# Attention: the swap of q's halves is begun before the store of the output three units old

## The chip, the cores and the metric

The kernel runs on one core of one Trainium2 chip. The metric is the device time of a whole execution in microseconds. Three runs of the kernel before took 2433.12, 2435.80 and 2437.37 us, so its median is 2435.8 us.

## The reference, cut to what matters

The input is x of shape 8 x 512 x 512. A layer norm goes ahead of each of two layers, and both are added to their input. The first is an attention with 16 heads of 128 columns, the second a feed-forward layer that works on the 128 best rows of every 1024. The change touches only the attention, of which these lines matter:

```python
q = _rope((x @ Wq).reshape(b, n, H, HD)); k = _rope((x @ Wk).reshape(b, n, H, HD))
v = (x @ Wv).reshape(b, n, H, HD)
# _rope, with t1, t2 = t[..., :half], t[..., half:]
return jnp.concatenate([t1 * cos - t2 * sin, t1 * sin + t2 * cos], axis=-1)
o = o_cmp * g_cmp[..., None] + o_slc * g_slc[..., None] + o_swa * g_swa[..., None]
return o.reshape(b, n, H * HD) @ Wo
```

In these inputs all 8 key blocks of a row are chosen, so the chosen attention is the causal one.

## The kernel before, in words

The work is cut into 128 units. A unit is one head of one batch: its 512 rows lie along the free axis and the 128 columns of the head on the partitions. `unit(p, k, j)` numbers them: pair p of heads (8 of them), 4 groups k, 4 units j in each.

A unit passes through a pipeline of three bodies on each engine; every engine has its program written out in this order.

- TensorE (`body`, L618): projects q and k of unit u (L600, 12 matmuls of 512 columns each), then computes the scores of unit u-1 (L643), turns the probabilities of unit u-2 (L657), projects v (L613) and multiplies the probabilities of u-2 with v into bank 6 (L678).
- ScalarE (`body`, L754): `output_out(u)` copies that product, which is unit u-3's output by the time it does so, from bank 6 into `o_sb` (L737). `evacuate(u, 0)` copies q from its bank into `s_full[0]` (L706); later `evacuate(u, 1)` does the same with k. Between these it mixes the probabilities (L743) and takes v (L751). After them come the exponentials, and two roundings into `qk_hi` (L713).
- SyncE (`body`, L492) issues the transfers. `swap(u, 0)` (L466) waits until q is in `s_full[0]` (L468) and writes its lower half of 64 partitions to the upper half of `s_swap[0]` (L469) and the upper to the lower (L470). `swap(u, 1)` does so for k. `store` (L472) waits for `output_out` (L479) and writes `o_sb` to `o_scratch` in DRAM (L480). Loads of weights, of v's weights and of gates go in at a few units in each pair of heads.
- GpSimd (`body`, L565): `turn(u, 0)` waits for q's swap and makes the rotation: times cosine (L555), swapped times sine (L556), sum (L559). `turn(u, 1)` does it for k. Then `low` (L563) makes the two low parts, q's first. These `qk_lo` and `qk_hi` are what the scores read one unit later.
- VectorE reads the scores, masks them, mixes the probabilities (L847, L863) and makes low parts.

One buffer is shared: `o_sb = s_swap[1]` (L401). The output is copied into the same tile that k's swap fills afterwards. So SyncE waits, between the store and k's swap, until the store has landed (`out_slot_free`, L505). Also, `evacuate(u, 0)` on ScalarE waits until GpSimd has made q's low part of unit u-1 (`lo_done[0]`, L705), since both use `s_full[0]`.

All transfers are issued by SyncE on one queue, whose packets go over 16 DMA engines. 125 units (3 to 127) have a store and both swaps. Units 0 to 2 have no store, and after unit 127 only stores are left.

Of the kernel before, what the change touches and what calls it, by code (L numbers as in the profile page):

```python
# [371 lines left out]
def attend(nc, phase, banks, m, gates, gates_full, xt_hi, xt_lo, weights, rope_d, misc_d, o_dram, gates_dram, chunks):  # L372
# [75 lines left out]
    def unit(p, k, j):  # L448

        return p * PAIR + k * 4 + j  # L450
# [12 lines left out]
    with nc.Block() as block:  # L463
        @block.sync
        def _(sp):
            def swap(u, k):  # L466

                sp.wait_ge(evacuated[k], u + 1)  # L468
                sp.dma_start(s_swap[k][0:64, :], s_full[k][64:128, :]).then_inc(swapped[k], 16)  # L469
                sp.dma_start(s_swap[k][64:128, :], s_full[k][0:64, :]).then_inc(swapped[k], 16)  # L470

            def store(p, k, j):  # L472

                u = unit(p, k, j)
                if j < 3:
                    p, k = (p, k - 1) if not (isinstance(k, int) and k == 0) else (p - 1, 3)
                    j += 4
                j -= 3
                sp.wait_ge(out_evacuated, u - 1)  # L479
                sp.dma_start(o_dram[bass.ds(p * PAIR + k * 2 + (j % 2) * B + j // 2, 1)].rearrange("o p n -> p (o n)"), o_sb[:])\  # L480
                    .then_inc(out_slot_free, 16)

            def load_gates(p):

                if isinstance(p, int) and p == 0:
                    sp.dma_start(gates[:, 1:PAIR], gates_dram[:, 1:PAIR]).then_inc(gates_loaded, 16)
                    return
                sp.wait_ge(win_step, (p * PAIR - 1) * 2)
                n = 1 if isinstance(p, int) and p == PAIRS else PAIR
                sp.dma_start(gates[:, 0:n], gates_dram[:, bass.ds(p * PAIR, n)]).then_inc(gates_loaded, 16)  # L490

            def body(p, k, j, project=True, output=True, gate=False, ahead=False, split=False):  # L492
                u = unit(p, k, j)
                if output:
                    store(p, k, j)
                if project:
                    swap(u, 0)
                if gate:
                    load_gates(p)
                if split is not False:  # L500
                    sp.wait_ge(projected[0], split * PAIR - 1 + j % 2)
                    weights.load(sp, split, 0, j % 2)
                if project:
                    if output:
                        sp.wait_ge(out_slot_free, (u - 2) * 16 + 16)  # L505
                    swap(u, 1)
                if split is not False:
                    sp.wait_ge(projected[1], split * PAIR - 1 + j % 2)
                    weights.load(sp, split, 1, j % 2)
                if ahead is not False:  # L510
                    weights.load_v(sp, ahead)

            def quad(p, k, first=False, ahead=False, split=False):
                body(p, k, 0, gate=first)
                body(p, k, 1, ahead=ahead)
                body(p, k, 2, split=split)
                body(p, k, 3, split=split)

            def middle(p):
                for k in range(1, 3):  # L520
                    quad(p, k)

            sp.dma_start(causal[:], misc_d[:, MISCW:MISCW + P]).then_inc(causal_loaded, 16)
            sp.dma_start(rope[:].rearrange("p a n -> p (a n)"), rope_d).then_inc(rope_loaded, 16)
            body(0, 0, 0, output=False)
            sp.wait_ge(zeros_set, 4)
            sp.dma_start(gates_dram[:, 1:1 + U], gates_full[:].rearrange("p u r t -> p u (r t)")).then_inc(gates_stored, 16)
            body(0, 0, 1, output=False)
            sp.wait_ge(gates_stored, 16)
            load_gates(0)  # L530
            body(0, 0, 2, output=False, ahead=1)
            body(0, 0, 3)
            middle(0)
            quad(0, 3, split=1)
            for p in range(1, PAIRS - 1):
                quad(p, 0, first=True, ahead=p + 1)
                middle(p)
                quad(p, 3, split=p + 1)
            quad(PAIRS - 1, 0, first=True)
            middle(PAIRS - 1)  # L540
            quad(PAIRS - 1, 3)
            body(PAIRS, 0, 0, project=False, gate=True)
            sp.wait_ge(projected[2], U)
            chunks.load_first(sp, 0)
            body(PAIRS, 0, 1, project=False)
            body(PAIRS, 0, 2, project=False)
            sp.wait_ge(out_slot_free, 16 + 16 * U)
# [1133 lines left out]
```

## Time and profile before

| | |
|---|---|
| median of three runs | 2435.8 us |
| the profiled execution, its own time | 2433.43 us |
| its span | 2431.6 us |
| TensorE busy | 2350.1 us (97%) |
| VectorE busy | 1913.1 us (79%) |
| GpSimd busy | 1588.7 us (65%) |
| ScalarE busy | 1521.4 us (63%) |
| granted TensorE clock, mean | 0.991 of full speed |

The span is 1.8 us shorter than the execution's own time. The attention lies between about 75 and 1815 us. Busy shares are means over the span; the rows below show a single unit in order of time. In a timeline row the first number is the start, the second the duration, then engine, line, operation, what is written and read, and in brackets for how long the engine had been idle and who released it. "SPq" is the queue of SyncE: its duration is the time that issuing a transfer takes, not the transfer.

### The profile page before, as it was taken

The page shows a single profiled execution, that of the slowest core. Times are in us where ns is not written, and L with a number is a line of the kernel's source. Part 1 is how long each engine was busy: PE and PEld are TensorE (multiplying, and loading weights), DVE is VectorE, ACT ScalarE, POOL GpSimd, SP SyncE. Part 2 cuts the span into 40 slices and gives each one's busy share as a digit, 9 for nine tenths or more (in the row PEclk, how much of TensorE's full clock was granted, in tenths as well). Part 3 has the DMA queues.
Part 4 walks back from the last instruction along what each step waited for, and adds up shares of the span by engine and source line. Part 5 has one row for each costly group of instructions (what it writes and reads, how often), then busy time and mean ns, then how long its engine had stood idle before and what let it go on. Part 6 is the DMA issues. An engine that isn't in the chain of part 4 may idle for free. (4 is left out here: it accounts for less than half of the span.)

```text
span 2431.6 us, 42771 instructions
## 1 busy us (share of the span) xinstructions
PE 2350.1 (97%) x13456; PEld 2067.5 (85%) x13456; DVE 1913.1 (79%) x6101; ACT 1521.4 (63%) x4192; POOL 1588.7 (65%) x1206
## 2 busy tenths in 40 slices
PE   6899999999999999999999999999969999999998
PEld 5799899989888998998999898889967888887776
DVE  7489898988888898988889888889864777775223
ACT  7577777777777777777777777777753222213442
POOL 1677877787787778778777877877744333433442
PEclk9999999999999999999999999999989999999999
DMA  5212222232222222222212222222225334332266
GB/s 169 73 53 66 72 75 62 66 83 55 66 72 75 54 74 78 60 62 76 75 53 75 76 62 60 78 56 63 62 99 187 121 103 154 139 104 87 97 184 221
DMA packets 143214, 215.44 MB, mean 89 GB/s; under 512 B 15136, under 2 KB 53408, under 8 KB 141984
## 3 DMA queue, kind: packets, MB, share of 16 engines
q1 hardware_dynamic: 143008, 212.95, 29.5%
q8 instruction: 99, 1.62, 0.3%
q14 instruction: 107, 0.88, 0.1%
HBM read 94.66 MB, written 51.12 MB: 60 GB/s over the span
## 5 line engine op out<-in xcount | busy, mean ns | idle before, releaser
L555 POOL TENSOR_TENSOR s_full<-s_full,rope 128x512 f32<-128x512 f32 x256 | 334.8, 1308 | 340.3 <-DMA s_swap<-s_full 340.0
L559 POOL TENSOR_TENSOR s_full<-s_full,s_swap 128x512 f32<-128x512 f32 x256 | 331.3, 1294 | 36.7
L556 POOL TENSOR_TENSOR s_swap<-s_swap,rope 128x512 f32<-128x512 f32 x256 | 331.2, 1294 | 0.0
L563 POOL TENSOR_TENSOR qk_lo<-s_full,qk_hi 128x512 fp32r<-128x512 f32 x256 | 326.5, 1296 | 0.0
L718 ACT ACTIVATE pt_hi<-bank 128x384 fp32r<-128x384 f32 (+1 forms) x384 | 174.9, 528 | 221.4 <-PE bank L657 221.0
L1015 POOL TENSOR_TENSOR o_lo<-o_raw,o_hi 128x2048 fp32r<-128x2048 f32 x32 | 149.6, 4675 | 241.7 <-ACT o_hi L1129 202.1
L613 PE MATMUL bank<-wv_hi,xt_hi 128*128 128x256 f32 x1024 | 300.2, 293 | 0.0
L724 ACT ACTIVATE bank<-bank,shift 128x512 f32<-128x512 f32 (+3 forms) x512 | 256.7, 501 | 58.9 <-DVE bank L829 58.3
L613 PE MATMUL bank<-wv_hi,xt_lo 128*128 128x256 f32 x1024 | 289.9, 283 | 0.0
L613 PE MATMUL bank<-wv_lo,xt_hi 128*128 128x256 f32 x1024 | 289.8, 283 | 0.0
L829 DVE TENSOR_REDUCE bank<-bank 128x8 f32<-128x512 f32 (+3 forms) x512 | 253.1, 494 | 0.0
L825 DVE TENSOR_REDUCE shift<-bank 128x1 f32<-128x512 f32 (+3 forms) x512 | 246.4, 481 | 0.0
L847 DVE SCALAR_TENSOR_TENSOR bank<-bank,coef,cb 128x192 f32<-128x192 f32 (+1 forms) x512 | 195.5, 405 | 50.4 <-ACT probs L743 50.3
L730 ACT ACTIVATE win<-win,shift 128x192 f32<-128x192 f32 (+1 forms) x512 | 225.5, 440 | 0.0
L713 ACT ACTIVATE qk_hi<-s_full 128x512 fp32r<-128x512 f32 x256 | 161.3, 630 | 83.5 <-POOL s_full L559 78.7
L600 PE MATMUL bank<-xt_hi,wq_hi 128*128 128x512 f32 x512 | 208.5, 407 | 3.4 <-PEq L193 3.4
L1191 PE MATMUL bank<-wo_hi,o_hi 128*128 128x512 f32 x512 | 204.6, 400 | 5.8 <-PEq L463 3.3
L839 DVE TENSOR_TENSOR pt_lo<-bank,pt_hi 128x384 fp32r<-128x384 f32 (+1 forms) x384 | 207.0, 595 | 1.1 <-ACT pt_hi L718 1.1
L600 PE MATMUL bank<-xt_hi,wq_lo 128*128 128x512 f32 x512 | 200.9, 392 | 0.0
L1191 PE MATMUL bank<-wo_hi,o_lo 128*128 128x512 f32 x512 | 200.0, 391 | 0.0
L1191 PE MATMUL bank<-wo_lo,o_hi 128*128 128x512 f32 x512 | 199.8, 390 | 0.0
L600 PE MATMUL bank<-xt_lo,wq_hi 128*128 128x512 f32 x512 | 199.4, 389 | 0.0
(181 smaller groups left out, 7028.3 us busy)
## 6 DMA issues: line engine op xcount, KB each, us to landing
s_swap<-s_full SPq DMA_DIRECT2D x512, 128.0 KB, 2.3
o_scratch<-s_swap SPq DMA_DIRECT2D x128, 256.0 KB, 2.0
o_raw<-o_scratch SPq DMA_DIRECT2D x32, 1024.0 KB, 6.2
w_raw<-in_L_ffn_W SPq DMA_DIRECT2D x64, 256.0 KB, 3.0
xin<-in_L_attn_x SPq DMA_DIRECT2D x14, 1024.0 KB, 5.6
base_scratch<-x SPq DMA_DIRECT2D x8, 1024.0 KB, 4.7
base<-base_scratch SPq DMA_DIRECT2D x32, 256.0 KB, 4.3
out<-base SPq DMA_DIRECT2D x32, 256.0 KB, 3.6
```

The source lines that it names most:

```text
L555: nc.gpsimd.tensor_tensor(s_full[k][:], s_full[k][:], rope[:, 0, :], ALU.mult).then_inc(cos_done[k], 1)
L556: nc.gpsimd.tensor_tensor(s_swap[k][:], s_swap[k][:], rope[:, 1, :], ALU.mult).then_inc(sin_done[k], 1)
L559: nc.gpsimd.tensor_tensor(s_full[k][:], s_full[k][:], s_swap[k][:], ALU.add).then_inc(roped[k], 1)
L563: nc.gpsimd.tensor_tensor(qk_lo[k][:], s_full[k][:], f32(qk_hi[k][:]), ALU.subtract).then_inc(lo_done[k], 1)
L600: last = nc.tensor.matmul(banks[QK_BANK[k]][:, :], w[k][s][:, c, :], v[:, b, c, :], start=(n == 0), stop=(n == 3 * C - 1))
L613: last = nc.tensor.matmul(out, x[:, b, c, at:at + P], w[:, c, :], start=(n == 0), stop=(n == 3 * C - 1), skip_group_check=True)
L724: nc.scalar.activation(n, n, ACT.Exp, bias=shift1[:, t:t + 1], scale=-1.0, accum_out=sums[:, 1, t:t + 1]).then_inc(exp_row, 1)
L730: nc.scalar.activation(win[:, t, lo:], win[:, t, lo:], ACT.Exp, bias=shift2[:, t:t + 1], scale=-1.0, accum_out=sums[:, 2, t:t + 1]).then_i ...
L825: nc.vector.tensor_reduce(shift1[:, t:t + 1], n[:, 0:(t + 1) * P], AX.X, ALU.min)
L829: nc.vector.reduce_sum(sc[:, t, 0:nb], n[:, 0:nb * BS].rearrange("p (n s) -> p n s", s=BS), AX.X).then_inc(row_read, 1)
L839: nc.vector.tensor_tensor(pt_lo[:, PTOFF[g]:PTOFF[g] + w], banks[PT_BANK[g]][:, 0:w], f32(pt_hi[:, PTOFF[g]:PTOFF[g] + w]), ALU.subtract). ...
L1191: last = nc.tensor.matmul(banks[t][:, :], o[k % 2][:, g, t * P:(t + 1) * P], w[:, k * G + g, :], start=(k == 0 and n == 0), stop=(k == K - ...
```

## The change

On SyncE, in the body of a unit, both half-swaps of q stand ahead of the store of the output. Nothing else is changed: the same instructions with the same waits are issued, in another order on this one engine. The wait for the store's landing stays where it was, ahead of k's swap. It acts in the 125 units that have both; the loads of gates, of weights and of v's weights keep their places behind the pair.

```diff
             def body(p, k, j, project=True, output=True, gate=False, ahead=False, split=False):
                 u = unit(p, k, j)
+                if project:
+                    swap(u, 0)
                 if output:
                     store(p, k, j)
-                if project:
-                    swap(u, 0)
                 if gate:
                     load_gates(p)
```

## Rows read from the trace of the kernel before

**Rows 1.** Page, part 1: busy time, share of the span and instructions.

```profile
PE 2350.1 (97%) x13456; PEld 2067.5 (85%) x13456; DVE 1913.1 (79%) x6101; ACT 1521.4 (63%) x4192; POOL 1588.7 (65%) x1206
```

**Rows 2.** Timeline of PE: first score matmul of six units.

```profile
118.31 0.22 PE L643 MATMUL bank<-qk_hi,qk_hi 128*128 128x128 f32 x1
...
624.37 0.22 PE L643 MATMUL bank<-qk_hi,qk_hi 128*128 128x128 f32 x1
637.83 0.22 PE L643 MATMUL bank<-qk_hi,qk_hi 128*128 128x128 f32 x1
...
1012.71 0.22 PE L643 MATMUL bank<-qk_hi,qk_hi 128*128 128x128 f32 x1
1025.97 0.22 PE L643 MATMUL bank<-qk_hi,qk_hi 128*128 128x128 f32 x1
...
1774.93 0.22 PE L643 MATMUL bank<-qk_hi,qk_hi 128*128 128x128 f32 x1
```

**Rows 3.** Timeline of ScalarE, one unit: output copied, q evacuated.

```profile
1009.48 0.59 ACT L737 ACTIVATE s_swap<-bank 128x512 f32<-128x512 f32 x1
1010.19 0.60 ACT L706 ACTIVATE s_full<-bank 128x512 f32<-128x512 f32 x1
```

**Rows 4.** Timeline of SyncE's queue, the same unit: store, q's swap, k's second half.

```profile
1010.10 0.34 SPq L480 DMA_DIRECT2D o_scratch<-s_swap  x1
1010.82 0.46 SPq L469 DMA_DIRECT2D s_swap<-s_full  x1
1011.32 0.60 SPq L470 DMA_DIRECT2D s_swap<-s_full  x1
1014.09 0.60 SPq L470 DMA_DIRECT2D s_swap<-s_full  x1
```

**Rows 5.** Timeline of GpSimd: the unit before's end, q's and k's turn, low parts.

```profile
1008.44 2.55 POOL L563 TENSOR_TENSOR qk_lo<-s_full,qk_hi 128x512 fp32r<-128x512 f32 x2
1013.82 1.29 POOL L555 TENSOR_TENSOR s_full<-s_full,rope 128x512 f32<-128x512 f32 x1 [2.84 <-DMA s_swap<-s_full]
...
1017.75 1.30 POOL L555 TENSOR_TENSOR s_full<-s_full,rope 128x512 f32<-128x512 f32 x1
```

**Rows 6.** Sources L480, L470: time from issue to landing of their transfers.

```profile
DMA to landing us min/median/max: 2.0/2.0/3.2
DMA to landing us min/median/max: 2.3/2.4/4.3
```

**Rows 7.** Page, part 6: other transfers, KB each, median us to landing.

```profile
out<-base SPq DMA_DIRECT2D x32, 256.0 KB, 3.6
wk_raw<-in_L_attn_Wk SPq DMA_DIRECT2D x16, 256.0 KB, 3.2
```

**Rows 8.** Timeline, first unit of a pair: SyncE's queue, GpSimd's k.

```profile
717.06 0.36 SPq L480 DMA_DIRECT2D o_scratch<-s_swap  x1
717.55 0.47 SPq L469 DMA_DIRECT2D s_swap<-s_full  x1
718.07 0.60 SPq L470 DMA_DIRECT2D s_swap<-s_full  x1
718.71 0.58 SPq L490 DMA_DIRECT2D gates<-gates_scratch  x1
...
724.82 1.30 POOL L555 TENSOR_TENSOR s_full<-s_full,rope 128x512 f32<-128x512 f32 x1
```

**Rows 9.** GpSimd around a late landing of q's swap.

```profile
613.60 1.29 POOL L555 TENSOR_TENSOR s_full<-s_full,rope 128x512 f32<-128x512 f32 x1 [3.80 <-DMA s_swap<-s_full]
...
626.50 1.27 POOL L555 TENSOR_TENSOR s_full<-s_full,rope 128x512 f32<-128x512 f32 x1 [2.47 <-DMA s_swap<-s_full]
...
639.39 1.28 POOL L555 TENSOR_TENSOR s_full<-s_full,rope 128x512 f32<-128x512 f32 x1 [2.46 <-DMA s_swap<-s_full]
```

**Rows 10.** DMA queues, window 611 to 613 us: packets, MB, share of 16 engines.

```profile
q8 instruction: 1, 0.02, 3.7%
```

**Rows 11.** GpSimd, k's cosine after a late landing of k's swap.

```profile
871.39 1.30 POOL L555 TENSOR_TENSOR s_full<-s_full,rope 128x512 f32<-128x512 f32 x1 [0.33 <-DMA s_swap<-s_full]
```

## The prediction

> **What bounds the kernel now.** I began with the page's busy shares [rows 1]: TensorE is busy for 97% of the span, and no other engine reaches 80%. Then I read, in TensorE's timeline, the first score matmul of each unit, which marks where TensorE is in its program [rows 2]. From 1012.71 to 1025.97 is 13.26 us, and this distance repeats in most units: it is what TensorE's own instructions take back to back. From unit 1 at 118.31 to unit 125 at 1774.93 there are 124 distances and 1656.62 us; 124 x 13.25 is 1643.0. So all stalls of TensorE in the attention together are 13.6 us. More than that no reordering on SyncE can win there, and it can lose only what outgrows the room around TensorE.
>
> That room is read from the other engines in one ordinary unit. ScalarE copies the output from 1009.48 to 1010.07 and takes q from 1010.19 to 1010.79 [rows 3]. SyncE issues the store at 1010.10 and is through at 1010.44; q's swap begins at 1010.82, 0.03 after ScalarE has finished q [rows 4]. GpSimd waits for that swap until 1013.82, then does q's cosine, sine and sum, and reads k's swap at 1017.75 [rows 5]. Its last low part of the unit before ended at 1008.44 + 2.55 = 1010.99, and TensorE asks for it at 1012.71 [rows 2, 5]: 1.72 us of room.
>
> GpSimd has a loop of its own. q can be taken only when q's low part of the unit before is made, and GpSimd starts only after q is taken and swapped. Where it is behind, that loop shows its own length: 626.50 to 639.39 is 12.89 us [rows 9]. Against 13.26 it has 0.37 us of room per unit. Whatever makes q or k late on GpSimd by less is caught up; by more, in every unit, GpSimd becomes the bound.
>
> **The change part by part.** Nothing is added or removed; two issues change places with one, in 125 units.
>
> *q's swap.* Does it start earlier? Before, SyncE had finished the store's issue 0.38 us before q's swap began (1010.44, 1010.82) [rows 4]. What it waited for was ScalarE. In the tightest kind of unit, the first of a pair, where ScalarE takes q right behind the output, the store's issue ends at 717.42 and the swap begins at 717.55 [rows 8]. So there is no delay for the change to remove: gain 0 us in issue. A gain or loss in transfer: q's second half lands 2.4 us after issue at the median, 2.3 at the least [rows 6]. With no store ahead it could be 0.1 sooner; a queue behind it could make it a little later. Either is inside the 0.37 of GpSimd's loop. I take 0.
>
> *The store.* It moves behind the swap. A third issue in a row starts 0.64 us after the second (718.07, 718.71) [rows 8]. In the ordinary unit that is 1011.32 + 0.64 = 1011.96 in place of 1010.10: 1.86 us later. Nothing reads the store itself soon: ScalarE wants the tile back one unit later. Its landing is what k's swap waits for.
>
> *k's swap.* The store lands 2.0 us after issue at the median and 3.2 at most [rows 6]; now it stands behind two half-swaps. Below, 2.0. Above, 3.2, which is also the median of a 256 KB load issued right behind k's half-swaps (wk_raw), or even 3.6 of the stores at the kernel's end [rows 7]. I take 2.2, since each half-swap lands at the same distance as alone or within 0.1 to 0.2 us of it. Then the store lands at 1014.16, k's first half is issued at 1014.19 and the second 0.50 later at 1014.69, where it was 1014.09 [rows 4]: 0.60 us later. It lands 2.4 later, at 1017.09. GpSimd wants it at 1017.75 [rows 5], so 0.66 us of cover is left of some 1.3. With 2.0 the cover is 0.86. With 3.2 k lands at 1018.09, 0.34 too late, and GpSimd's loop is 12.89 + 0.34 = 13.23, still just under 13.26. With 3.6 it is 0.74 late, the loop is 13.63, and 0.37 x 125 = 46 us are lost. The point from which it decides is a landing of 3.2 us.
>
> The Trainium skill has a rule that speaks against the change: in "DMA: Bandwidth & Descriptors", section "Queues, rings and completion order", a transfer's semaphore increment lands only after every earlier write of the same DMA engine. By that the store, now behind q's swap, can't be reported before 1011.32 + 2.4 = 1013.72. My 1014.16 is beyond that already, so the rule alone would leave the sum as it is. The trace before has no store in that place, so it neither agrees nor disagrees.
>
> *Units with a load between.* In the first unit of a pair the gates are issued at 718.71 [rows 8]. Now the store takes that slot, lands at 720.91, and k's second half goes out at 721.44, or some 0.3 later if the issue is held back by the long row of transfers. Landed by 724.2, it is read at 724.82. Covered. The load of weights or gates is issued 0.4 us later and is used much later.
>
> *Late landings.* Now and then a swap lands late. GpSimd waited 3.80 us instead of about 2.45 in front of 613.60 [rows 9], and one packet of instruction fetch, 0.02 MB, ran in that stretch; it took 3.7% of 16 engines x 2 us = 1.2 us of one engine [rows 10]. Nine units in the attention show late q of this size; each costs TensorE 0.2 to 0.45 us a unit on, as 13.46 for 13.26 (624.37 to 637.83) [rows 2]. These stay. Late k's are nearly covered: nine times GpSimd waits at k's cosine, for 0.18 to 0.41 us [rows 11]. With k 0.60 later these become about 0.9, still less than the 1.35 that cost 0.2. I take 0.1 us each: +1 us.
>
> Sum: 0 + 0 + 1 = +1 us on the profiled execution's own 2433.43 (span 2431.6 and 1.8 around it): 2434.4. The median of the runs is 2.4 above the profiled one, 2435.8, and by it the forecast is 2436.8 us.
>
> **The rivals.**
>
> *A: the queue delays the store.* The store behind q's swap lands after 3.2 us or more, and k's late landing becomes GpSimd's loop. For it: wk_raw and the last stores [rows 7]. Against it: those loads go in smaller packets or in a crowded stretch, while the half-swaps show next to nothing from standing behind one another [rows 6]. At 3.6 us: +46, 2482 us; at 3.3, with late landings that are no longer caught up, +10 to +25.
>
> *B: the fetches now hit more.* TensorE's late landings come from a fetch that meets a swap. k now has half its cover, and the store is a third transfer in the chain of waits. If the nine late k's cost as much as a late q does, and as many late stores join them, that is 18 x 0.44 = +8 us: 2443.8 us. For it: the 1.3 us of cover that just held k's today is 0.66 then. Against it: TensorE's 1.72 us of room behind GpSimd's end, and that a lateness of 1.35 costs only 0.2.
>
> *C: a quieter queue under q's swap.* If a store or fetch ahead of q's swap is what makes it late, with the store gone from there the late q's go. Of TensorE's 13.6 us of stalls I put about half down to late q's (nine, each with one or two slow units behind it) and the rest to the units where a new pair's weights are prepared on ScalarE and GpSimd, which the change leaves alone. So at most -7, say -6: 2429.8 us. Against it: the store has landed at 1012.10, before the first half-swap's data do, and the fetches stay.
>
> *D: the change doesn't do what it says.* This is what I hold for true: q's swap begins at the same time as before. It is part of the forecast.
>
> **How the numbers follow.** Forecast (nothing that can be told from the same) 0.74, A 0.08, B 0.12, C 0.06. A measurement of this kernel tells about 0.2% from no change, which is 4.9 us. Of the forecast's 0.74 I give 0.03 to an end above +4.9 and 0.02 to one below -4.9. Slower: 0.03 + 0.08 + 0.12 = 0.23. Faster: 0.02 + 0.06 = 0.08. Same: 0.69. The range goes down to 2431, the lower part of C left out, and up to 2446, which holds B and the mildest of A; the rest of A, above it, and C's full size below are the 2 in 10 left out.
>
> **What would show it.** In the changed kernel's SyncE timeline: q's swap still 0.03 us behind ScalarE's copy of q; the store 1.1 us behind its start; k's second half 0.4 to 0.9 us later than before. On GpSimd: the wait in front of q's cosine unchanged, about 2.8 in ordinary units; no regular wait in front of k's. On TensorE: 13.26 us from unit to unit. It would be wrong if that distance grew, if GpSimd waited at k's cosine in most units (A), if single units of 13.6 us became twice as many (B), or if waits of 3.8 us and more for q's swap disappeared (C).

## The result, and the profile after

Fourteen runs of the changed kernel, beside fourteen of the one before, gave a median of 2442.1 us (2438.1 to 2449.7) against 2435.9. The ratio is 1.0024, with a 95% interval of 1.0014 to 1.0034. A second comparison gave 2439.1 against 2435.0, ratio 1.0012 (1.0003 to 1.0020). So the change costs 3 to 6 us. Both intervals lie above 1, but the effect is only one to two tenths of a per cent.

The profiled execution took 2442.0 us for a span of 2440.2, 8.6 more than the span before. Where do they lie? These are first score matmuls in TensorE's timeline of the changed kernel, to be held against [rows 2].

```profile
122.18 0.22 PE L643 MATMUL bank<-qk_hi,qk_hi 128*128 128x128 f32 x1
...
1019.90 0.22 PE L643 MATMUL bank<-qk_hi,qk_hi 128*128 128x128 f32 x1
1033.16 0.22 PE L643 MATMUL bank<-qk_hi,qk_hi 128*128 128x128 f32 x1
...
1783.59 0.22 PE L643 MATMUL bank<-qk_hi,qk_hi 128*128 128x128 f32 x1
```

The first stands 3.9 us later than before (118.31), ahead of any unit that the change touches; in a second profile of the same kernel it is at 119.18, so this part is not the change's. From the first to the last row are 1661.4 us where there were 1656.6: the attention is 4.8 us longer. What follows it took the same (2440.2 - 1783.6 = 656.6; before 2431.6 - 1774.9 = 656.7). The ordinary unit is still 13.26 us.

The transfers of one ordinary unit on SyncE's queue, against [rows 4]:

```profile
1018.35 0.46 SPq L469 DMA_DIRECT2D s_swap<-s_full  x1
1018.85 0.60 SPq L470 DMA_DIRECT2D s_swap<-s_full  x1
1019.49 0.59 SPq L480 DMA_DIRECT2D o_scratch<-s_swap  x1
1022.02 0.46 SPq L469 DMA_DIRECT2D s_swap<-s_full  x1
1022.53 0.60 SPq L470 DMA_DIRECT2D s_swap<-s_full  x1
```

q's swap still begins 0.03 us after ScalarE has finished its copy of q (1017.72 + 0.60 = 1018.32):

```profile
1017.72 0.60 ACT L706 ACTIVATE s_full<-bank 128x512 f32<-128x512 f32 x1 [0.20 <-POOL qk_lo L563]
```

The store is issued 0.64 us behind q's second half, as forecast. But its issue takes 0.59 us in place of 0.34, and k's swap starts 2.53 us after it. From q's second half to k's second half are 3.68 us; before, 1014.09 - 1011.32 = 2.77. k is 0.91 us later in this unit, not 0.60; by the medians of the 125 units it is 0.99 (3.69 for 2.70). The sources L480 and L470 give the landings, against [rows 6]:

```profile
DMA to landing us min/median/max: 2.0/2.5/4.3
DMA to landing us min/median/max: 2.3/2.5/4.3
```

The store needs 2.5 us where it needed 2.0. The halves of L470 need 2.5 where they needed 2.4. This view has q's and k's second halves together; taken apart, q's went from a median of 2.37 to 2.50 us and k's stayed at 2.38. This small number turned out to matter. GpSimd's timeline, against [rows 5] and [rows 9]:

```profile
1008.45 1.27 POOL L555 TENSOR_TENSOR s_full<-s_full,rope 128x512 f32<-128x512 f32 x1 [2.55 <-DMA s_swap<-s_full]
...
1021.50 1.29 POOL L555 TENSOR_TENSOR s_full<-s_full,rope 128x512 f32<-128x512 f32 x1 [2.62 <-DMA s_swap<-s_full]
...
1034.54 1.28 POOL L555 TENSOR_TENSOR s_full<-s_full,rope 128x512 f32<-128x512 f32 x1 [2.61 <-DMA s_swap<-s_full]
```

GpSimd's cosine starts 0.13 us after the landing. From the issue of q's second half (1018.85) to the cosine (1021.50) are 2.65 us; before, 1013.82 - 1011.32 = 2.50. By the medians of all units it is 2.64 for 2.51: 0.13 us later, 0.15 in this unit. And where GpSimd is behind and runs at its own pace, its loop is now 13.05 us, where it was 12.89. The room under TensorE's 13.26 fell from 0.37 to 0.21 us a unit.

By which way does lateness on GpSimd reach TensorE? The prediction looked at TensorE's first score matmul, which has 1.72 us of room. The trace shows another way, here in the kernel before, one unit behind a late q (GpSimd had waited 4.35 us for it, until 573.58):

```profile
582.87 0.60 ACT L706 ACTIVATE s_full<-bank 128x512 f32<-128x512 f32 x1 [0.20 <-POOL qk_lo L563]
584.39 0.75 DVE L847 SCALAR_TENSOR_TENSOR bank<-bank,coef,cb 128x192 f32<-128x192 f32 x2 [1.02 <-ACT probs L743]
585.50 0.19 PEld L643 LDWEIGHTS bank<-qk_hi,qk_hi 128*128 128x128 f32 x1 [0.51 <-DVE probs L863]
```

ScalarE's copy of the next q waits for GpSimd's low part. Its mixing of probabilities stands behind that copy and is late too, VectorE waits 1.02 us for it, and the third of TensorE's four score groups waits for VectorE. The first score matmul at 584.24 was on time, yet the next one came 13.61 us later. I compared every unit, matmul by matmul, with an ordinary one: 10.6 of TensorE's 12.4 us of stalls before arise at this third group, and 14.7 of 17.2 in the changed kernel. TensorE's waits of 0.15 us and more for VectorE there, before and after (in total, times, longest):

```profile
PE bank L643 <- DVE probs L863: 5.2, 7, 1.2
PE bank L643 <- DVE probs L863: 7.7, 9, 1.3
```

One place where more stalls are seen is a stretch in which several things came late. The first score matmuls behind the last new pair, first of the kernel before, then of the changed one:

```profile
1587.92 0.22 PE L643 MATMUL bank<-qk_hi,qk_hi 128*128 128x128 f32 x1
...
1615.77 0.22 PE L643 MATMUL bank<-qk_hi,qk_hi 128*128 128x128 f32 x1
1629.03 0.22 PE L643 MATMUL bank<-qk_hi,qk_hi 128*128 128x128 f32 x1
...
1708.63 0.22 PE L643 MATMUL bank<-qk_hi,qk_hi 128*128 128x128 f32 x1
```

```profile
1595.19 0.22 PE L643 MATMUL bank<-qk_hi,qk_hi 128*128 128x128 f32 x1
...
1622.68 0.30 PE L643 MATMUL bank<-qk_hi,qk_hi 128*128 128x128 f32 x1
1636.39 0.23 PE L643 MATMUL bank<-qk_hi,qk_hi 128*128 128x128 f32 x1
...
1717.29 0.22 PE L643 MATMUL bank<-qk_hi,qk_hi 128*128 128x128 f32 x1
```

From the first row to the last are nine units in both. Before they take 120.71 us: two units are slow (14.14 and 13.71), one takes 13.30 and six take 13.26. Now they take 122.10 and all nine are over 13.3 us. This alone does not single out q's steady delay, for GpSimd also meets a late q there at 1679.7 (a wait of 3.66 us) that the kernel before did not have, and waits in front of k up to 0.66 us. The other place are the seven first units of a pair after the first, in which TensorE waits for VectorE's probabilities: together 99.8 us before and 101.7 now.

The short waits of GpSimd for a swap, those under 1.2 us, were 16 with 4.8 us in the attention, and are 32 with 13.0 us. In front of k's cosine stand 9 of them before (2.5 us) and 26 now (10.8 us). So both candidates are visible in the trace: q's landing, 0.13 to 0.15 us later in the ordinary unit, and k's swap, 0.91 to 0.99 us later with less cover.

### The profile page after: what moved, and what is told of

Its sections match the earlier page's. It is cut to its first block and busy times, and to the rows that moved or that the text cites. A ratio compares the mean times of both kernels' runs of the same rounds, so it can differ in the third digit from the quotient of the medians.

```text
span 2440.2 us, 42771 instructions
## 1 busy us (share of the span) xinstructions
PE 2354.2 (96%) x13456; PEld 2069.8 (85%) x13456; DVE 1907.3 (78%) x6101; ACT 1524.3 (62%) x4192; POOL 1588.8 (65%) x1206
```

## The experiments

Theory Q: what costs is q's landing, behind which the store now follows at once; it lengthens GpSimd's loop. Theory K, the kin of rival B: what costs is k's late start, which takes the cover from late landings. All ratios are to the kernel before on the same chip, in brackets the 95% interval.

**k late alone** (k_late). The old order, k's swap held back:

```diff
                         sp.wait_ge(out_slot_free, (u - 2) * 16 + 16)
+                        sp.wait_ge(scores_ready, (u - 1) * T + 3)
                     swap(u, 1)
```

> The order of the kernel before, with one more wait on SyncE: k's swap is issued only after the third of the four score matmul groups of the unit before, about 0.9 us later than now, which is by how much the change moved it. The store stays ahead of q's swap. Theory K (the change costs because k's swap starts 0.9 us later, so late landings find too little cover in front of GpSimd's k): slower than before by 4 to 6 us, as the change was; short waits of GpSimd at k's cosine in some 25 units instead of 9, slow units of TensorE as in the change. Theory Q (the change costs because the store behind q's swap makes q land 0.15 us later and lengthens GpSimd's own loop from 12.89 to 13.05 us): k's lateness is covered in nearly all units, the time is that of before within 2 us, GpSimd's loop stays at 12.89.

Measured: 2436.9 us, ratio 1.0001 (0.9993 to 1.0010). SyncE's timeline shows that k did start late, in this unit 3.67 us behind q's second half, as in the change:

```profile
1053.62 0.60 SPq L470 DMA_DIRECT2D s_swap<-s_full  x1
1056.79 0.46 SPq L469 DMA_DIRECT2D s_swap<-s_full  x1
1057.29 0.60 SPq L470 DMA_DIRECT2D s_swap<-s_full  x1
```

By the median of the units k is less late than in the change: 3.37 us behind q's second half, where the change has 3.69 and the kernel before 2.70. GpSimd's short waits came out as in the change: 30 with 13.9 us. Its loop stayed at 12.9. Theory K wanted 4 to 6 us; measured are 0.7, and the interval ends at 2.4. So K alone is not the cause; a microsecond or two from it is not ruled out.

**The change's order without the wait for the store** (own_after). The output gets a place of its own, the tail of `pt_lo`, so k's swap is not held:

```diff
-    o_sb = s_swap[1]
+    o_sb = Region(nc, phase + 4 * (2 * PTW - N))("o_sb", [P, N])
...
                 if project:
-                    if output:
-                        sp.wait_ge(out_slot_free, (u - 2) * 16 + 16)
                     swap(u, 1)
...
                 dve.wait_ge(pt_hi_done, (u - 2) * 3 + g + 1)
+                if g == 1:
+                    dve.wait_ge(out_slot_free, (u - 2) * 16 + 16)
```

> The order of the change (q's swap, then the store), but the output is copied to a place of its own (the tail of the low probabilities' tile, free at that time), so k's swap no longer waits for the store's landing; VectorE waits for it before it writes that tail, some 2 us later. Theory K: k's swap is again issued when ScalarE has k, and the time returns to that of before (2436) or just under it. Theory Q: q still lands 0.15 us late behind the store, GpSimd's loop is 13.05, and the time stays near that of the change (2440 to 2442). If both count, about half.

Measured: 2437.2 us, ratio 1.0009 (0.9999 to 1.0019), which tells nothing clearly by itself; it lies between K's 2436 and Q's 2440 to 2442. In the profile the short waits are back to 13 with 4.6 us, yet GpSimd's loop is 13.0. From the first score matmul at 118.82 to that of the last unit are 1674.6 us, no less than in the change (1673.5, counted from 122.18). That does not settle it either: the profiled execution took 2439.96 us, 2.7 more than this kernel's median, and one unit took 16.47 us where it took 14.17 before. It is the unit in which the timeline of GpSimd shows a new lateness, where a load of weights goes out between store and k's swap:

```profile
498.06 1.29 POOL L553 TENSOR_TENSOR s_full<-s_full,rope 128x512 f32<-128x512 f32 x1 [1.40 <-DMA s_swap<-s_full]
```

Its k had been issued at 491.76 and 492.27, right behind the weights' load at 491.12, and landed 5.4 us later, the longest of all half-swaps in that run.

**The control** (own_before): the same place of its own, with the old order.

> The order of the kernel before (store, then q's swap), with the output in a place of its own and no wait of k's swap for the store. It is the control of the run with the change's order: neither q nor k starts at another time than before, as the store had landed 1.5 us before k's swap was issued. Both theories: the time of before within 2 us. If the place itself cost something (VectorE's wait, another bank of memory), it would show here.

Measured: 2437.0 us, ratio 1.0000 (0.9991 to 1.0009); loop 12.9, short waits 14 with 5.0 us. The place costs nothing, and the wait of k's swap for the store cost nothing in the old order.

**The store last** (own_last): own place, and `store` behind `swap(u, 1)`.

> The output in a place of its own, and the store issued behind k's swap, last in the unit. q's swap has nothing right behind it or ahead of it; k's swap has the store behind it. Theory Q: GpSimd's loop is 12.89 or less and the time that of before or 1 to 2 us less, since k, not q, is disturbed and has 1.3 us of cover. Theory K: the same, since k's swap is issued early. Both expect no loss; a loss of 4 us or more would mean that the store's place in the queue matters in another way (VectorE waiting for its landing, 1016.4 against a landing at about 1017.2 in the ordinary unit, is the likely one).

Measured: 2510.0 us, ratio 1.0302 (1.0289 to 1.0316). Neither theory's number, but the place of the loss is the one named as likely. It is VectorE, waiting for the landing before it may write the tail, from the list of its waits:

```profile
DVE pt_lo L839 <- DMA o_scratch<-o_sb: 114.0, 112, 2.6
```

1.0 us in each of 112 units. So the time says nothing on q and k. The landings do say something: with the store right behind k's swap it is k's second half that lands late, 2.52 us after its issue at the median instead of 2.38, while q's is at 2.37. The store goes with a late landing of the half it follows, q's or k's.

**The changed kernel again** (after_again).

> The changed kernel itself, beside the others on one chip, so that they are compared with it directly. Both theories: 5 to 7 us above before.

Measured: 2439.1 us against 2435.0, ratio 1.0012 (1.0003 to 1.0020), less than expected. Its profile repeats the first: loop 13.0, 30 short waits with 12.4 us, 1673.4 us from the first score matmul at 119.18 to that of the last unit, as against 1673.5 in its first profile and 1668.5 before, counted alike.

**q late by waits** (q_slow). In `swap`, for q only:

```diff
                 sp.wait_ge(evacuated[k], u + 1)
+                if slow:
+                    for done in (lo_done[0], cos_done[0], sin_done[0], roped[0]):
+                        sp.wait_ge(done, u)
```

> The order of the kernel before; SyncE has four more waits, all fulfilled already, between the one for q on ScalarE and the first half-swap of q, in the 125 units with a store. They are meant to start q's swap 0.1 to 0.3 us later with nothing else in the queue, as the store behind it made it land 0.15 us later in the change. Theory Q (the length of GpSimd's own loop, q taken to q taken, is what counts): the loop goes from 12.89 to 13.0 to 13.2, lateness is caught up more slowly, and the time rises by 1 to 4 us, k's swap being on time. Theory K (k's start alone): the time of before within 2 us. Should the waits take no time on SyncE, GpSimd's loop stays at 12.89 and the run says nothing.

Measured: 2435.8 us, ratio 0.9996 (0.9987 to 1.0004). The trace shows that the four waits were carried out ahead of the one for q, so q's swap started at its usual time and the loop stayed at 12.9. As said ahead of the run, it tells nothing of Q; it does show what two kernels with the same timing differ by.

**Both** (q_slow_k_late).

> The four fulfilled waits ahead of q's swap and the wait of k's swap for the third score group together; store still ahead of q's swap. That puts both swaps where the change puts them while the store stays where it was. If the change costs by both together (a loop of 13.05 that leaves only 0.2 us a unit to catch up, and late landings of k that are no longer covered), this kernel is slower than before by 5 to 7 us, as the change is, though k's lateness alone cost nothing (k_late: 1.0001). If the store's place in the queue matters in another way than by q's and k's landing, it is within 3 us of before.

Measured: 2437.2 us, ratio 1.0003 (0.9994 to 1.0012). As q was not delayed, it is k_late a second time, and agrees with it: loop 12.9, 26 short waits with 13.0 us, k issued 3.31 us behind q's second half at the median, no loss that can be told. Against q_slow on the same chip, which differs by k's lateness alone, it is 1.4 us slower by the medians, less than the intervals tell.

**The store between the swaps** (own_mid): own place, the store taken from behind q's swap and issued when k is ready.

```diff
+                if output:
+                    if project:
+                        sp.wait_ge(evacuated[1], u + 1)
+                    store(p, k, j)
                 if project:
                     swap(u, 1)
```

> The output in its own place, and the store issued when k is ready, right ahead of k's swap: nothing stands behind q's swap until it has nearly landed, k's swap is issued 0.4 to 0.6 us later than before and has the store ahead of it. Theory Q: the loop is back at 12.89 and the time is that of before within 2 us. Theory K: k is as late as it is in the change by two thirds, so up to 4 us slower. VectorE needs the store landed by about 1016.5 in the ordinary unit, it lands at about 1015.7: covered except for late landings, at most 2 us.

Measured: 2436.1 us, ratio 1.0006 (0.9997 to 1.0015). The loop is back at 12.9 and the short waits stay (30 with 13.0 us). By Q within 2 us of before: it is (1.2 by the medians). K's 4 us are not reached, but k was issued only 2.87 us behind q's second half at the median, 0.17 later than before and not the 0.4 to 0.6 expected.

**A small transfer ahead of q's swap** (tiny_ahead), old order:

```diff
+                    if output:
+                        sp.wait_ge(evacuated[0], u + 1)
+                        sp.dma_start(tiny[bass.ds(u, 1)], rope_d[0:1, 0:16]).then_inc(tiny_done, 16)
                     swap(u, 0)
```

> The order of the kernel before, with one added transfer of 64 bytes (DRAM to DRAM, used by nobody) issued right ahead of q's swap once q is ready, in 125 units. Its issue takes SyncE 0.35 to 0.5 us, so q's swap starts that much later and nothing else moves; k's swap is not delayed. Theory Q (GpSimd's loop from q to q is what a delay of q's landing eats): the loop grows from 12.89 to 13.25 to 13.4 us, at or over TensorE's 13.26; late landings are never caught up, and the kernel is slower by 12 to 40 us. Theory K (only k's start counts): within 3 us of before, since q's delay leaves k more cover.

Measured: 2495.7 us, ratio 1.0251 (1.0237 to 1.0265). SyncE's and GpSimd's timelines:

```profile
1044.54 0.52 SPq L502 DMA_DIRECT2D tiny<-in_rope  x1
1045.11 0.59 SPq L472 DMA_DIRECT2D s_swap<-s_full  x1
1045.74 0.60 SPq L473 DMA_DIRECT2D s_swap<-s_full  x1
```

```profile
1048.24 1.29 POOL L562 TENSOR_TENSOR s_full<-s_full,rope 128x512 f32<-128x512 f32 x1 [3.16 <-DMA s_swap<-s_full]
...
1061.83 1.29 POOL L562 TENSOR_TENSOR s_full<-s_full,rope 128x512 f32<-128x512 f32 x1 [3.17 <-DMA s_swap<-s_full]
```

q's second half is issued 1.20 us behind the small transfer's start, where it was 0.50 behind the first half's: 0.70 us late, more than the 0.35 to 0.5 that I had reckoned, since the first half's issue behind another takes longer as well. The loop is 12.89 + 0.70 = 13.59 by that, and 1061.83 - 1048.24 = 13.59. TensorE follows it: the median of its units is 13.61 us, and 64 of 124 take 13.5 to 13.65. (13.59 - 13.26) x 125 = 41 of the 62 us lost, which is more than the 12 to 40 expected. The rest was not taken apart: late landings that nothing catches up any more would do it, and so would the added transfer itself, behind which the loads of weights land late (4.3 us at the median for 3.1), as in the next run. That a late q sets the pace once the loop is over 13.26 is shown by the 41 us; K has no place for them. It is a dose about five times the change's, on the other side of 13.26.

**The same behind q's swap** (tiny_behind).

> The same 64-byte transfer issued right behind q's swap, where the change has the store of 256 KB; the store stays ahead. It tells what of the store makes q land 0.15 us late. If any third transfer in the queue does it: GpSimd's loop is 13.0 to 13.1 and the kernel 2 to 4 us slower than before. If the store's data do it, by sharing the 16 DMA engines with the second half-swap: the loop stays at 12.9 and the time at that of before.

Measured: 2448.6 us, ratio 1.0061 (1.0047 to 1.0075). Neither expectation: the loop stayed at 12.9 and q's second half at 2.38 us, so a mere third transfer in the queue does not delay q; but the kernel lost 15 us otherwise. The loads of weights (source L137) landed far later behind this transfer, at first in the kernel before, then here:

```profile
DMA to landing us min/median/max: 2.8/3.1/7.1
```

```profile
DMA to landing us min/median/max: 4.5/4.9/6.9
```

k's swap behind such a load was late too (0.57 us of waiting in front of 934.77, 2.2 at the most; 34 waits with 24.5 us in front of k where there were 9 with 2.5). Six of the seven first units of a pair took 14.8 to 15.3 us instead of 14.1 to 14.7, the seventh 16.4. So waits in front of k do cost time when they are long enough. Why a transfer of 64 bytes from DRAM to DRAM holds up what follows it, I did not find out.

Nor is it the store's size alone that delays q. The kernel before already has loads of 256 KB right behind q's second half, those of wq in 14 units, and q's half lands there 2.40 us after its issue at the median; in front of the gates' 96 KB it lands after 2.37, as with nothing behind it. Of the transfers that stand right behind a second half in these traces, only those from SBUF to DRAM go with a late landing: the store to `o_scratch` (2.50 in 122 swaps of the changed kernel, 2.51 in 113 of own_last) and the single one to `gates_scratch` (2.52 before). What about such a store does it was not tried.

**The change's order with k held** (own_after_k_late): own_after, and k_late's wait.

> The output in its own place, the store right behind q's swap, and k's swap held back to the third score group: q's late landing and k's late start together again, without the wait for the store's landing. Own place with the change's order alone measured 1.0009, k late alone 1.0001. If both together make the change's loss: 1.0012 to 1.0024, above own_after. If q's landing makes it alone: 1.0009 again, and GpSimd's waits in front of k (13 us in all) cost nothing.

Measured: 2436.1 us against 2433.3, ratio 1.0014 (1.0005 to 1.0023). Loop 13.0. It lies in the range of the first expectation, and above own_after by less than either interval; k was issued 3.34 us behind q's second half at the median. Its profile does not repeat the loss: 1667.9 us from the first score matmul at 120.36 to that of the last unit, no more than before (1668.5). That profile is of an execution of 2433.45 us, 2.6 below this kernel's median.

**q's second half from ScalarE** (act_half), a try at a better version. SyncE issues the second half for k only; on ScalarE:

```diff
+                if k == 0:
+                    act.wait_ge(evacuated[0], u + 1)
+                    act.dma_start(s_swap[0][64:128, :], s_full[0][0:64, :]).then_inc(swapped[0], 16)
```

> A try at a better version than both: the order of the kernel before, and q's second half-swap issued by ScalarE itself, right behind its copy of q, so that both halves go out at once instead of 0.5 us apart. Theory Q: GpSimd's loop falls from 12.89 to 12.4 to 12.6, late landings are caught up within two units, up to 3 us faster. But ScalarE pays for issuing, some 0.5 us a unit; where it is the last (the first units of a pair, slow units of 14.2 us) that shows directly, some 8 x 1 us, so it may come out even or 5 us slower. Theory K says nothing of it beyond ScalarE's price.

Measured: 2466.4 us, ratio 1.0130 (1.0115 to 1.0146). ScalarE's and GpSimd's timelines:

```profile
1045.88 0.60 ACT L707 ACTIVATE s_full<-bank 128x512 f32<-128x512 f32 x1
1046.51 0.49 ACTq L711 DMA_DIRECT2D s_swap<-s_full  x1
1047.05 1.29 ACT L747 ACTIVATE probs<-bank,cb,coef 128x64 f32<-128x64 f32 x4 [0.57 <-ACT s_full L707]
```

```profile
1049.51 1.29 POOL L556 TENSOR_TENSOR s_full<-s_full,rope 128x512 f32<-128x512 f32 x1 [2.63 <-DMA s_swap<-s_full]
```

Both halves went out at 1046.51, the second landed 2.86 us later, and GpSimd could start at 1049.51, after 3.0 us. From ScalarE's copy of q (1045.88) to the cosine are 3.63 us, exactly as before (1010.19 to 1013.82): issuing half a microsecond earlier gave nothing, GpSimd's loop did not fall to 12.4 to 12.6, and ScalarE paid 0.57 us. Of the 31 us lost against before, 20 lie in the seven first units of a pair, which took 119.6 us together instead of 99.8. No version that beats both was found.

**Taken together.** Nine comparisons differ from the kernel before only by where the store stands and how late k starts, or by the output's own place, which costs nothing (own_before). In the table the landing is that of q's second half after its issue, at the median; the waits are GpSimd's in front of k's cosine from 0.15 us on; the last column runs from the third unit's first score matmul to the last unit's, in the one execution profiled (before: 2.37, 9 with 2.5 us, 1668.5 us).

| run | q lands, us | waits in front of k | ratio | attention, us |
|---|---|---|---|---|
| own_before | 2.37 | 7, 2.6 us | 1.0000 | 1668.5 |
| q_slow | 2.37 | 6, 2.6 us | 0.9996 | 1670.4 |
| k_late | 2.37 | 26, 12.6 us | 1.0001 | 1669.8 |
| q_slow_k_late | 2.37 | 20, 10.7 us | 1.0003 | 1670.9 |
| own_mid | 2.37 | 24, 11.2 us | 1.0006 | 1671.7 |
| own_after | 2.50 | 7, 3.8 us | 1.0009 | 1674.6 |
| the change | 2.50 | 26, 10.8 us | 1.0024 | 1673.5 |
| after_again | 2.50 | 25, 11.7 us | 1.0012 | 1673.4 |
| own_after_k_late | 2.50 | 18, 8.1 us | 1.0014 | 1667.9 |

GpSimd's loop is 13.0 to 13.05 in the last four and 12.9 in the first five. Their mean ratios are 1.0015 and 1.0001, so the time goes with q's landing. But inside each group the runs with k late are, by their mean, the slower ones as well. The means of the four kinds are 0.9998 (neither late), 1.0003 (k late), 1.0009 (q late) and 1.0017 (both), or about -0.5, +1, +2 and +4 us. Estimated from the mean times of all these executions, the store behind q's swap costs 2.7 us (1.5 to 3.9, a 95% interval) and k's lateness 1.5 (0.2 to 2.7). The last column is of little help: kernels with the same timing (before, own_before, q_slow) differ in it by 1.9 us, and own_after_k_late goes the other way.

So the larger part of the loss goes with the store's place behind q's swap, and a smaller part probably with k's late start; Theory Q holds in the main, but not as the only cause. No run delayed q by 0.13 us with nothing behind it (q_slow was meant to), so that q's landing is how the store's place costs time is well supported by the loop and by tiny_ahead, not shown.

## Why the prediction came out as it did

The forecast of 2436.8 was low by 2 to 5 us, and the time of 2442.1 lies in the range of 2431 to 2446. The range went up that far for Rival B; the forecast proper, +1 us and nothing to be told from the same, is not what came: both intervals exclude no change, and the first comparison is 6.2 us up, beyond the 4.9 that the prediction took for telling. By its steps:

- *TensorE sets 13.26 us and no reordering wins more than the stalls.* The 13.26 us is right, and in the changed kernel the same. (The rows are the first scores of units 2 to 126, not 1 to 125, and with the measured 13.26 the stalls come to 1656.6 - 1644.2 = 12.4 us, not 13.6; in the changed kernel they are 17.2.)
- *The 1.72 us of room at TensorE's first score matmul.* True, but lateness does not enter there. It enters by ScalarE's copy of q and VectorE at the third score group, where most of the stalls arise before and after.
- *q's swap starts no earlier.* Right. In the changed kernel SyncE still waits for ScalarE's copy of q. The reordering takes nothing away from q's path (rival D as part of the forecast).
- *q's transfer: "either is inside the 0.37 of GpSimd's loop. I take 0."* This is the step that failed. The landing moved by 0.13 to 0.15 us, which is inside the 0.37, but room that is only partly used up is not free: runs with this landing cost 2 us and more where the term was 0. The reading is that late landings and a new pair's delays are repaid from this room, and repaid at 0.21 us a unit they reach TensorE in more units (29 units over 13.3 us for 22); no run isolated it.
- *The store lands 2.2 us after its issue, k is 0.60 late.* The bounds of 2.0 and 3.2 held for the median, the value was low: 2.5, and k 0.91 to 0.99 late, beyond the 0.4 to 0.9 given as a sign. By k_late it cost little: 0.7 us, at most 2.4 by its interval.
- *The rule of the Trainium skill* ("DMA: Bandwidth & Descriptors", section "Queues, rings and completion order") that a transfer's increment lands after every earlier write of its engine. The trace agrees: in all 125 units of the changed kernel the store landed at least 0.61 us after q's second half, and in the nine units where q's half took 3.5 to 4.3 us the store took 3.3 to 4.3 too. The rule speaks of the delay of the later transfer; the delay of the earlier one, q's, is what the runs show to count.
- *Late k's, +1 us.* The waits in front of k went from 9 to 26. Alone they gave +0.7 us in k_late, which a single comparison cannot tell from 0 or from 2; over all runs the estimate is 1.5.
- *Rival A*, a landing over 3.2 us at the median: did not come, 2.5; nine stores took longer.
- *Rival B* gave 2443.8 and is near the time, but for the most part not by its mechanism: the waits in front of k are there (9 to 26), but produced alone they cost 0.7 us, at most 2.4. That the range reached the time is in so far luck. Its sign, twice as many units of 13.6 us, did not come either: 18 units took over 13.5 us before, 20 in the first profile of the changed kernel and 24 in the second. What B says of the fetches is borne out by the trace before: a packet of instruction fetch runs during all nine late q's, and during only one other swap of q.
- *Rival C*: nine waits of 3.3 us and more for q remain, where there were ten. Of those of 3.8 us and more, C's own sign, four remain of nine, but q's second half still takes 3.5 us and more to land in nine of the units, as before. The store ahead was not what made them late.

## What to carry to other kernels

Before a transfer is moved behind another, look at who waits for the one in front: a store right behind it can push its landing too, here by 0.13 us, which no view of issue times shows. An engine whose own loop is a few per cent under the pace of the bound is not free either; its spare time repays irregular delays, so a small steady loss on it can cost a few stalls even though the bound's ordinary unit doesn't change. To find such a loop, take the distances between its iterations where the engine is behind, not the mean. And look for the place where the bound engine's stalls arise before you measure its room: here it was the third score group, not the first.

## What was not expected of the hardware

- A second half-swap of 128 KB with the 256 KB store from SBUF right behind it landed 2.50 us after issue at the median instead of 2.37; with 64 bytes right behind it 2.38, with a 256 KB load right behind it 2.40.
- The issue of the store on SyncE took 0.34 us alone and 0.59 as the third in a row; the first half-swap 0.46 alone and 0.59 behind another transfer.
- Of two half-swaps issued at the same moment from SyncE and ScalarE the later landed after 2.86 us. Issued 0.5 us apart from SyncE alone, the second landed 2.87 us after the first's issue.
- A 64-byte DRAM-to-DRAM transfer in the queue raised the median landing of the 256 KB loads from 3.1 to 4.9 us (tiny_behind).
- One packet of instruction fetch of 16 KB meeting a swap made it land 1.3 to 1.9 us later than the median of 2.37, in nine swaps of q in the kernel before.
